# Local-attention layers: third group of the first FFN product moved to the output's PSUM banks, and a turned probability unit copied behind each maximum

## The chip, the cores and the metric

The kernel runs on one NeuronCore of a Trainium2 chip. The metric is the device time of one launch in microseconds (us). Before the change it is 3528.7 us, the median of 3 runs (3528.33 to 3528.79).

## What is computed

The reference is a chain of two blocks over 8 sequences of 512 rows with 256 features: a Mamba branch and an FP4-quantized FFN on a layer norm of the input, then block-sparse attention and two local-attention layers on a layer norm of the result. The change touches the local-attention layers alone. Cut to that part:

```python
def _layer(x, wqkv, qs, ksc, wo, lg, lb, w1, b1, w2, b2):      # called for l = 0, 1
    q, k, v = split(shift_token(x) @ wqkv)                     # 8 heads of 64
    q, k = rotary_xpos(l2norm(q) * qs, l2norm(k) * ksc)
    o = local_attention(q, k, v)       # windows of 128 rows; each sees itself and the one before
    x = x + o @ wo
    h = layer_norm(shift_token(x)) * lg + lb
    a, g = split(h @ w1 + b1)                                  # 682 columns each
    return x + (a * gelu(g)) @ w2 + b2
```

## The kernel before

`local_attention_layers` writes every engine's program by hand and orders them with semaphores; nothing is scheduled by a tool. It works on one batch (512 rows, four tiles of 128) at a time: 2 layers x 8 batches are 16 passes of `body`. In 15 of them (`more` is true) the body also prepares the next batch `n`, from its projection to its first scores, between the steps of its own batch `it`. The sixteenth has no next batch.

**PSUM.** All eight banks (128 x 512 fp32 each) are taken: `ps_s` has four, `ps_t` two, `ps_o` two. `ps_s` holds scores, raw q and k and the first FFN product; `ps_t` holds transposes and the product with `wo`; `ps_o` holds v, the attention output and, as `ps_y`, the second FFN product.

**Attention.** A unit is two heads of one window of 128 queries: 16 units u in 8 pairs s. For each pair TensorE writes scores into bank u % 4 (`score`, L2241 and L2249), VectorE takes the negated row maximum (`maxima`, L1989), ScalarE the exponential with its row sum (`exponents`, L2124), VectorE the reciprocals of a pair's sums (`inverses`, L2007), GpSimd scales (`scale_rows`, L1884), TensorE turns the scaled unit into bank u % 2 of `ps_t` (`turn_p`, L2261), VectorE copies it to SBUF (`take_p`, L2015), and TensorE weighs v with it (`weigh`, L2280). Units with window 0 see 128 columns a head (units 0, 1, 8, 9, "narrow"), the others 256. The stages are staggered: in step s TensorE does `score(s)`, `turn_p(s-2)`, `weigh(s-3)`, and VectorE does `inverses(s-1)`, `maxima(s)` for units 2s and 2s+1, `take_p(s-2)` for units 2s-4 and 2s-3. `turn_p` of unit u waits until unit u-2 has been copied, since both use the same bank of `ps_t`. The first two pairs of a batch are scored in the body of the batch before.

**First FFN product.** After the layer norm (`hn`, turned to `hT`) comes the loop over j = 0 to 5 at L2357 to L2369. Group j is the product for 128 columns of a (`a`=0) and 128 of g (`a`=1); j = 5 holds the 42 columns that are left of both in one bank. `pair(j)` gives banks 2 and 3 of `ps_s` to even j and banks 0 and 1 to odd j. ScalarE takes gelu of the g half (L2177, L2180), VectorE adds the bias to the a half and multiplies (`hid`, L2073). Group j may therefore start only when `hid` of group j-2 is done:

```python
                for j in range(JC):
                    if j >= 2:
                        pe.wait_ge(hid_ready.s, hid_ready.at(it, j - 1))
```

From j = 2 on, TensorE follows each group with the transposes of one tile of the next batch's q and k (`turn_qk`, L2230), which ScalarE and VectorE copy out (`take_q` L2130, `take_k` L1982). Then follow half of the second FFN product (`down_rows`, L2292), the next batch's first scores, and the other half.

**VectorE around it.** Ahead of its first `hid` VectorE has the next batch's `rotate(n, 2)`, `rotate(n, 3)`, `squares(n, 2)`, `squares(n, 3)`. `squares` (L1975, L1978) writes the sums of squares; it waits until GpSimd's `inverse_norms` (a power, L1867) of the tile before has read them. GpSimd runs `turn_heads` (L1861), `inverse_norms` (L1867) and `scale_heads` (L1874) tile by tile.

Of the kernel before, what the change touches and what calls it, by code (L numbers as in the profile page):

```python
# [7 lines left out]
ALU = mybir.AluOpType  # L8
# [1639 lines left out]
def local_attention_layers(nc, io, W, stream, base_dram, out, NB):  # L1648
# [15 lines left out]
    with ExitStack() as ctx:  # L1664
# [118 lines left out]
        def nk(u):  # L1783
            return 1 if UNIT[u][0] == 0 else 2
# [4 lines left out]
        def layers(eng, first, body):  # L1789

            first(0)
            for l in range(L):
# [5 lines left out]
                else:  # L1798
                    body(l, NB - 1, l * NB + NB - 1, None, None)

        def halves(ap):
            return ap.rearrange("p (h d) -> p h d", h=NH)

# [134 lines left out]
        def _(dve):  # L1938
# [43 lines left out]
                dve.tensor_copy(kT[:, :, t * P:(t + 1) * P], ps_t[:, 1, :].rearrange("p (c n) -> p c n", c=IC))\  # L1982
                    .then_inc(kT_ready.s, 1)

            def maxima(it, s):
                for u in (2 * s, 2 * s + 1):
                    w = 2 * P * nk(u)
                    dve.wait_ge(scores.s, scores.at(it, u + 1))
                    dve.tensor_reduce(negmax[:, u, :], ps_s[:, u % 4, 0:w].rearrange("p (h n) -> p h n", h=2),  # L1989
                                      AX.X, ALU.max, negate=True).then_inc(max_ready.s, 1)  # L1990

            def masked_maxima(it, s):

# [12 lines left out]
                dve.wait_ge(exp_ready.s, exp_ready.at(it, 2 * s + 2))  # L2006
                dve.reciprocal(inv[:, 2 * s:2 * s + 2, :], den[:, 2 * s:2 * s + 2, :]).then_inc(inv_ready.s, 1)  # L2007

            def take_p(it, s):
                for u in (2 * s, 2 * s + 1):  # L2010
                    w = 2 * P * nk(u)
                    dve.wait_ge(p_turned.s, p_turned.at(it, u + 1))
                    if u >= 8:
                        dve.wait_ge(pv_done.s, pv_done.at(it, u // 2 - 3))
                    dve.tensor_copy(pt[:, u % 8, 0:w], ps_t[:, u % 2, 0:w]).then_inc(pt_ready.s, 1)  # L2015

            def first(it):
                for t in range(TT):
# [9 lines left out]
            def body(l, b, it, nl, nb):  # L2028
                n, more = it + 1, nl is not None
                for s in range(AHEAD, PAIRS + TURN_LAG):  # L2030
                    if s <= PAIRS:
                        inverses(it, s - 1)
                    if s < PAIRS:
                        maxima(it, s)
                    take_p(it, s - TURN_LAG)
                if more:
                    for t in range(2):
                        rotate(nl, n, t)
                        squares(n, t)

                dve.wait_ge(wo_done.s, wo_done.at(it, 1))
                dve.wait_ge(xr_in.s, xr_in.at(it, 16))
                dve.wait_ge(xa2_ready.s, xa2_ready.at(it, 0))
                dve.wait_ge(hn_ready.s, hn_ready.at(it, 0))
                for half in (slice(P, D), slice(0, P)):
                    dve.tensor_tensor(xa[:, :, half], ps_x[:, :, half], xr[:, :, half], ALU.add).then_inc(xa_ready.s, 1)

                st.turn(it)
                dve.wait_ge(xa_ready.s, xa_ready.at(it, 2))
                for t in range(TT):  # L2050
                    st.done(dve.bn_stats(stats[:, t, 0:6], xa[:, t, 0:P]))
                dve.wait_ge(shifted.s, shifted.at(it, 1))
                for t in range(TT):
                    st.done(dve.bn_stats(stats[:, t, 6:12], xsh[:, t, :]))
                dve.wait_ge(st.s, st.at(2 * TT))
                st.done(dve.memset(tick[:, :], 0.0))
                for t in range(TT):
                    dve.bn_aggr(mv[:, t, :], stats[:, t, :]).then_inc(mv_ready.s, 1)
                dve.wait_ge(rstd_ready.s, rstd_ready.at(it, 1))
                for t in range(TT):  # L2060
                    for half, src in enumerate((xa[:, t, 0:P], xsh[:, t, :])):
                        dve.tensor_scalar(hn[:, t, half * P:(half + 1) * P], src, mv[:, t, 0:1], rstd[:, t:t + 1],
                                          ALU.subtract, ALU.mult).then_inc(hn_ready.s, 1)
                if more:
                    rotate(nl, n, 2)
                    rotate(nl, n, 3)
                    squares(n, 2)
                    squares(n, 3)

                for j in range(JC):  # L2070
                    m = jj(j)
                    dve.wait_ge(gl_ready.s, gl_ready.at(it, j + 1))
                    dve.scalar_tensor_tensor(hid[0:m, j, :], ps_s[0:m, pair(j), :], b1_cols[0:m, l, 0, j:j + 1],  # L2073
                                             gl[0:m, j % 2, :], ALU.add, ALU.mult).then_inc(hid_ready.s, 1)
                    if more and j >= JC - TT:
                        take_k(n, j - JC + TT)
                if more:
                    for s in range(AHEAD):
                        masked_maxima(n, s)
                    inverses(n, 0)  # L2080
                dve.wait_ge(y_done.s, y_done.at(it, 1))
                dve.wait_ge(xa2_ready.s, xa2_ready.at(it, 1))
                dve.wait_ge(stored.s, stored.at(it, 0))
                dve.tensor_tensor(xo[:, :, :], ps_y, xa2[:, :, :], ALU.add).then_inc(xo_ready.s, 1)
                st.end()
# [4 lines left out]
        def _(act):  # L2090
# [53 lines left out]
            def body(l, b, it, nl, nb):  # L2144
                n, more = it + 1, nl is not None
                for s in range(AHEAD, PAIRS):
                    exponents(it, s)
                    if s == HALF + PV_LAG - 1:
                        take_o(it, 0)
                if more:  # L2150
                    take_x(n)
                    square(n, 0)
                take_o(it, 1)
                if more:
                    square(n, 1)
                if l == L - 1:
                    act.wait_ge(stored.s, stored.at(it, 0))
                    act.dma_start(xo[:, :, :], base_dram[b].rearrange("(t p) d -> p t d", p=P)).then_inc(base_in.s, 16)
                if more:
                    take_v(n, 0)  # L2160
                    take_v(n, 1)
                    square(n, 2)
                    take_v(n, 2)
                    square(n, 3)
                for k in range(DC):
                    act.wait_ge(h_turned.s, h_turned.at(it, k + 1))
                    act.activation(hT[:, k, :], ps_t[:, k, :], ACT.Identity, bias=ln_cols[:, l, k, 1:2],
                                   scale=ln_cols[:, l, k, 0:1]).then_inc(hT_ready.s, 1)
                if more:
                    take_v(n, 3)  # L2170
                for j in range(JC):
                    m = jj(j)
                    act.wait_ge(ag_proj.s, ag_proj.at(it, j + 1))
                    if j >= 2:
                        act.wait_ge(hid_ready.s, hid_ready.at(it, j - 1))
                    if j < JC - 1:
                        act.activation(gl[:, j % 2, :], ps_s[:, pair(j) + 1, :], ACT.Gelu, bias=b1_cols[:, l, 1, j:j + 1])\  # L2177
                            .then_inc(gl_ready.s, 1)
                    else:
                        act.activation(gl[0:m, j % 2, :], ps_s[64:64 + m, pair(j), :], ACT.Gelu, bias=b1_tail[64:64 + m, l, 1, JC - 1:JC])\  # L2180
                            .then_inc(gl_ready.s, 1)
                    if more and j >= JC - TT:
                        take_q(n, j - JC + TT)
                if more:
                    for s in range(AHEAD):
                        exponents(n, s)
                if l == L - 1:
                    act.wait_ge(xo_ready.s, xo_ready.at(it, 1))
                    act.dma_start(out[b].rearrange("(t p) d -> p t d", p=P), xo[:, :, :]).then_inc(stored.s, 16)
# [4 lines left out]
        def _(pe):  # L2194
# [116 lines left out]
            def body(l, b, it, nl, nb):  # L2311
# [42 lines left out]
                    project_v(n, 3)  # L2354
                pe.wait_ge(hT_ready.s, hT_ready.at(it, DC))
                for j in range(JC):
                    if j >= 2:  # L2357
                        pe.wait_ge(hid_ready.s, hid_ready.at(it, j - 1))
                    elif more:
                        pe.wait_ge(raw_ready.s, raw_ready.at(n, TT - 1 + j))  # L2360

                    for a in range(2 if j < JC - 1 else 1):
                        at = a * FULL + j * P if j < JC - 1 else 2 * FULL
                        for k in range(DC):
                            last = pe.matmul(ps_s[:, pair(j) + a, :], w_1[:, k, at:at + P], hT[:, k, :],  # L2365
                                             start=(k == 0), stop=(k == DC - 1))
                    last.then_inc(ag_proj.s, 1)
                    if more and j >= JC - TT:
                        turn_qk(n, j - JC + TT)  # L2369
                if more:  # L2370
                    pe.wait_ge(v_ready.s, v_ready.at(n, TT))
                down_rows(it, (0, 2))
                if more:
                    pe.wait_ge(qT_ready.s, qT_ready.at(n, TT))
# [93 lines left out]
```

## Time and profile before

| | |
|---|---|
| median of 3 runs | 3528.7 us |
| the profiled execution | 3527.94 us |
| its span | 3526.2 us |
| TensorE matmuls busy | 3201.3 us (91%) |
| TensorE weight loads busy | 1865.3 us (53%) |
| VectorE busy | 2495.2 us (71%) |
| ScalarE busy | 1764.6 us (50%) |
| GpSimd busy | 1581.5 us (45%) |

The local layers fill the span from about 2016 us on. Columns of a timeline row: start in us, duration in us, engine, line, operation, output<-input, shapes, count; in brackets the idle time of the engine just before, and what ended it. PE is TensorE's matmuls, PEld its weight loads, DVE VectorE, ACT ScalarE, POOL GpSimd. Every fp32 matmul or transpose of the program stands as two records. The end of a matmul in the records is modelled, its start is recorded.

### The profile page before, as it was taken

The numbers are of one execution on the slowest core, as the hardware profiler recorded it, in microseconds if no ns is written. First come the engines' busy times: TensorE is split into PE (matmuls) and PEld (weight loads), VectorE is DVE, ScalarE is ACT, GpSimd is POOL, SyncE is SP. The second block draws the span as 40 slices with busy tenths as digits, with TensorE's granted clock in tenths as the row PEclk, the third lists the DMA queues.
The fourth block names the chain that finished last, engine by engine and source line by source line (L and its number), as shares of the span: only waits on it lengthen the run. The fifth ranks groups of instructions, "written<-read, shape, count | busy, mean of one in ns | idle before, by whom it ended". The sixth has DMA issues, their size and how long they took to land. (4 is left out here: it accounts for less than half of the span.)

```text
span 3526.2 us, 50669 instructions
## 1 busy us (share of the span) xinstructions
PE 3201.3 (91%) x16204; PEld 1865.3 (53%) x16204; DVE 2495.2 (71%) x3778; ACT 1764.6 (50%) x4156; POOL 1581.5 (45%) x974
## 2 busy tenths in 40 slices
PE   1799999989999876999999889999999999999997
PEld 1245454444544433666666546665666566666655
DVE  6499999999999995777777555555555555555553
ACT  1585767768576751556655433333333333333332
POOL 0456666666666662000000064444555555555552
PEclk9899999999999998999999889999999999999999
DMA  1466666757666672211000000000001100000000
GB/s 51 155 225 223 227 237 216 253 205 238 222 225 238 215 268 89 73 34 36 24 24 18 31 1 18 18 18 18 18 18 36 48 25 24 24 24 19 23 18 18
DMA packets 146655, 343.31 MB, mean 97 GB/s; under 512 B 14898, under 2 KB 78470, under 8 KB 146582
## 3 DMA queue, kind: packets, MB, share of 16 engines
q1 hardware_dynamic: 138134, 334.02, 27.9%
q10 hardware_dynamic: 8448, 8.39, 0.7%
q8 instruction: 37, 0.61, 0.1%
q14 instruction: 36, 0.29, 0.0%
HBM read 320.87 MB, written 21.50 MB: 97 GB/s over the span
## 5 line engine op out<-in xcount | busy, mean ns | idle before, releaser
L581 POOL TENSOR_TENSOR hb<-bcB,du 128x1024 f32<-128x1024 f32 x256 | 601.3, 2351 | 318.0 <-DVE hb L681 278.6
L670 DVE TENSOR_TENSOR_SCAN ps_dA<-ps_dA,hb 128x1024 f32<-128x1024 f32 x256 | 585.8, 2288 | 62.7 <-ACT ps_dA L831 62.4
L1053 PE MATMUL ps_y<-hb,ident 128*128 128x512 f32 x1024 | 496.4, 613 | 71.0 <-DVE hb L681 71.0
L1884 POOL TENSOR_TENSOR c_pr<-c_pr,c_inv 128x512 f32<-128x512 f32 (+1 forms) x256 | 233.4, 933 | 396.5 <-DVE c_inv L2007 394.6
L1053 PEld LDWEIGHTS ps_y<-hb,ident 128*128 128x128 f32 x1024 | 188.2, 193 | 310.4 <-issue 183.7
L1418 ACT ACTIVATE b_pr<-b_ps_s,b_negmax 128x256 f32<-128x256 f32 (+1 forms) x512 | 263.8, 527 | 163.2 <-DVE b_negmax L1332 160.9
L2124 ACT ACTIVATE c_pr<-c_ps_s,c_negmax 128x256 f32<-128x256 f32 (+1 forms) x512 | 222.0, 449 | 228.1 <-DVE c_negmax L1989 153.1
L2365 PE MATMUL c_ps_s<-c_hT,c_w 128*128 128x512 f32 x704 | 319.3, 599 | 17.4 <-DVE c_hid L2073 16.6
L831 ACT ACTIVATE ps_dA<-delta,a_neg 128x511 f32<-128x511 f32 x512 | 330.1, 676 | 1.1
L681 DVE TENSOR_TENSOR hb<-ps_dA,bcC 128x1024 f32<-128x1024 f32 x256 | 312.1, 1219 | 6.1 <-issue 0.3
L1861 POOL TENSOR_TENSOR c_q_cos<-c_q_cos,c_q_sin 128x1024 f32<-128x1024 f32 x64 | 150.7, 2355 | 236.5 <-DVE c_q_sin L1968 236.5
L1332 DVE TENSOR_REDUCE b_negmax<-b_ps_s 128x2 f32<-128x512 f32 (+1 forms) x320 | 204.2, 681 | 70.6 <-PE b_ps_s L1489 69.6
L1276 POOL TENSOR_TENSOR b_xb<-b_xb,b_o_bias 128x1024 f32<-128x1024 f32 x8 | 18.8, 2346 | 495.8 <-DMA b_xb<-x_scratch 495.8
L2211 PE MATMUL c_ps_s<-c_w_qkv,c_xT 128*128 128x512 f32 x512 | 237.9, 608 | 0.7 <-ACT c_xT L2097 0.7
L2365 PEld LDWEIGHTS c_ps_s<-c_hT,c_w 128*128 128x128 f32 x704 | 128.3, 191 | 175.4 <-issue 144.4
L1503 PE MATMUL b_ps_t<-ident,b_pr 128*128 128x128 f32 x1280 | 189.2, 285 | 24.7 <-DVE b_pt L1354 12.7
L2073 DVE SCALAR_TENSOR_TENSOR c_hid<-c_ps_s,c_b_cols,c_gl 128x512 f32<-128x512 f32 x96 | 70.3, 745 | 185.9 <-ACT c_gl L2177 166.3
L1867 POOL TENSOR_TENSOR c_rn<-c_ssc,c_mhalf 128x16 f32<-128x16 f32 x64 | 186.2, 2910 | 33.8 <-DVE c_ssc L1978 33.4
L2103 ACT ACTIVATE c_sq<-c_ps_s 128x512 f32<-128x512 f32 x128 | 69.5, 595 | 255.2 <-PE c_ps_s L2211 255.2
L1503 PEld LDWEIGHTS b_ps_t<-ident,b_pr 128*128 128x128 f32 x1280 | 136.6, 141 | 113.7 <-DVE b_pt L1354 55.6
L1489 PE MATMUL b_ps_s<-b_kf,b_qm 32*128 32x256 f32 (+1 forms) x1024 | 177.0, 459 | 0.9 <-ACT b_kf L1391 0.9
L2177 ACT ACTIVATE c_gl<-c_ps_s,c_b_cols 128x512 f32<-128x512 f32 x80 | 55.1, 689 | 238.8 <-PE c_ps_s L2365 238.8
(241 smaller groups left out, 6320.7 us busy)
## 6 DMA issues: line engine op xcount, KB each, us to landing
bcB<-bc_scratch SPq DMA_DIRECT2D x256, 512.0 KB, 4.4
bcC<-bc_scratch SPq DMA_DIRECT2D x256, 512.0 KB, 4.6
c_x<-stream_scratch SPq DMA_DIRECT2D x16, 512.0 KB, 5.3
c_xr<-stream_scratch SPq DMA_DIRECT2D x16, 512.0 KB, 4.2
xn<-in_x_dram SPq DMA_DIRECT2D x8, 512.0 KB, 5.1
xr<-in_x_dram SPq DMA_DIRECT2D x8, 512.0 KB, 5.1
x_scratch<-xr SPq DMA_DIRECT2D x8, 512.0 KB, 7.0
b_x<-x_scratch SPq DMA_DIRECT2D x8, 512.0 KB, 4.3
```

The source lines that it names most:

```text
L581: pool.tensor_tensor(hb[:, s % RING, :, :], bcB[:, s % ROWS, :, :], bc(du[:, c % 2, :].unsqueeze(1), [P, NG, T]), ALU.mult)\
L670: dve.tensor_tensor_scan(flat(h_all), flat(h_all), flat(tile), 0.0, ALU.mult, ALU.add)\
L681: dve.tensor_tensor(tile, h_all, bcC[:, s % ROWS, :, :], ALU.mult).then_inc(weighed.s, 1)
L831: last = act.activation(dA[:, s % 2, n, 1:], delta[:, c, 1:], ACT.Exp, scale=a_neg[:, c, g * NG + n:g * NG + n + 1])
L1053: last = pe.matmul(ps_y[:, :], W["ident"][:, :], hb[:, r % RING, i, :], start=False, stop=(g == GROUPS - 1 and i == terms - 1))
L1332: dve.tensor_reduce(negmax[:, u, 0:heads], ps_s[:, u % 4, :].rearrange("p (h n) -> p h n", h=heads), AX.X, ALU.max, negate=True).then_inc( ...
L1418: last = act.activation(pr[:, u % 8, cols], ps_s[:, u % 4, cols], ACT.Exp, bias=negmax[:, u, i:i + 1], accum_out=den[:, qt, h:h + 1])
L1503: last = pe.transpose(ps_t[:, u % 2, k * P:(k + 1) * P], pr[:, u % 8, k * P:(k + 1) * P], W["ident"][:, :])
L1884: pool.tensor_tensor(rows, rows, bc(inv[:, u, :].unsqueeze(2), [P, 2, w]), ALU.mult)\
L2124: last = act.activation(pr[:, u % 6, i * w:(i + 1) * w], ps_s[:, u % 4, i * w:(i + 1) * w], ACT.Exp, scale=-1.0 if s < AHEAD else 1.0, bia ...
L2211: last = pe.matmul(ps_s[:, pair(t) + a, :], xT[:, k, t * P:(t + 1) * P], w_qkv[:, k, a * INNER:(a + 1) * INNER], start=(k == 0), stop=(k = ...
L2365: last = pe.matmul(ps_s[:, pair(j) + a, :], w_1[:, k, at:at + P], hT[:, k, :], start=(k == 0), stop=(k == DC - 1))
```

## The change

Two edits, both in the local layers.

1. A helper `ag(j, a)` names the bank of each group. j = 2 goes to the two banks of `ps_o`; the later groups move up by one in the alternation over `ps_s`. With it go the waits: j = 2 waits for the next batch's v to be out of `ps_o` (`v_ready`, a wait that stood ahead of the second product) and for no `hid`; j = 3, 4, 5 wait for `hid` of groups 0, 1, 3; the second product waits for `hid` of group 2.
2. VectorE's two maxima and two copies of a step are interleaved: maximum 2s, copy 2s-4, maximum 2s+1, copy 2s-3.

```diff
+        def ag(j, a):
+
+            return ps_o[:, a, :] if j == 2 else ps_s[:, pair(j + (j > 2)) + a, :]
+
...
                 for s in range(AHEAD, PAIRS + TURN_LAG):
                     if s <= PAIRS:
                         inverses(it, s - 1)
-                    if s < PAIRS:
-                        maxima(it, s)
-                    take_p(it, s - TURN_LAG)
+                    for i in range(2):
+                        if s < PAIRS:
+                            maximum(it, 2 * s + i)
+                        take_p(it, 2 * (s - TURN_LAG) + i)
...
-                    dve.scalar_tensor_tensor(hid[0:m, j, :], ps_s[0:m, pair(j), :], b1_cols[0:m, l, 0, j:j + 1],
+                    dve.scalar_tensor_tensor(hid[0:m, j, :], ag(j, 0)[0:m, :], b1_cols[0:m, l, 0, j:j + 1],
...
-                        act.activation(gl[:, j % 2, :], ps_s[:, pair(j) + 1, :], ACT.Gelu, bias=b1_cols[:, l, 1, j:j + 1])\
+                        act.activation(gl[:, j % 2, :], ag(j, 1), ACT.Gelu, bias=b1_cols[:, l, 1, j:j + 1])\
...
                 for j in range(JC):
-                    if j >= 2:
-                        pe.wait_ge(hid_ready.s, hid_ready.at(it, j - 1))
+
+                    if j >= 3:
+                        pe.wait_ge(hid_ready.s, hid_ready.at(it, (1, 2, 4)[j - 3]))
+                    elif more and j == 2:
+                        pe.wait_ge(v_ready.s, v_ready.at(n, TT))
                     elif more:
                         pe.wait_ge(raw_ready.s, raw_ready.at(n, TT - 1 + j))
...
-                            last = pe.matmul(ps_s[:, pair(j) + a, :], w_1[:, k, at:at + P], hT[:, k, :],
+                            last = pe.matmul(ag(j, a), w_1[:, k, at:at + P], hT[:, k, :],
...
-                if more:
-                    pe.wait_ge(v_ready.s, v_ready.at(n, TT))
+                pe.wait_ge(hid_ready.s, hid_ready.at(it, 3))
                 down_rows(it, (0, 2))
```

TensorE, first FFN product in the body's loop, groups j = 1 to 3 before (`c_hT` is the normed input turned, `c_w` the weights, `c_raw` the semaphore of `rotate`):

```order
L2365 MATMUL c_ps_s<-c_hT,c_w 128x512 [waits c_raw]
L2365 MATMUL c_ps_s<-c_hT,c_w 128x512 x3
L2358 ISA
L2365 MATMUL c_ps_s<-c_hT,c_w 128x512 [waits c_hid]
L2365 MATMUL c_ps_s<-c_hT,c_w 128x512 x3
L2230 MATMUL c_ps_t<-ident,c_qr 128x128 [waits c_qr_ready]
L2230 MATMUL c_ps_t<-ident,c_qr 128x128 x7
L2358 REGISTER_ALU
L2365 MATMUL c_ps_s<-c_hT,c_w 128x512 [waits c_hid]
```

and in the changed kernel:

```order
L2371 MATMUL c_ps_s<-c_hT,c_w 128x512 [waits c_raw]
L2371 MATMUL c_ps_s<-c_hT,c_w 128x512 x3
L2371 MATMUL c_ps_o<-c_hT,c_w 128x512 [waits c_v_ready]
L2371 MATMUL c_ps_o<-c_hT,c_w 128x512 x3
L2233 MATMUL c_ps_t<-ident,c_qr 128x128 [waits c_qr_ready]
L2233 MATMUL c_ps_t<-ident,c_qr 128x128 x7
L2362 ISA
L2371 MATMUL c_ps_s<-c_hT,c_w 128x512 [waits c_hid]
```

The wait for `hid` has moved from group 2 to group 3; the number of matmuls and their order are the same.

VectorE, attention, step s = 7 of the body's loop before (units 14 and 15 get their maximum, units 10 and 11 are copied):

```order
L2007 RECIPROCAL c_inv<-c_den 128x4 [waits c_exp]
L1988 REGISTER_ALU
L1989 TENSOR_REDUCE c_negmax<-c_ps_s 128x2 [waits c_scores]
L1988 REGISTER_ALU
L1989 TENSOR_REDUCE c_negmax<-c_ps_s 128x2 [waits c_scores]
L2014 REGISTER_ALU [waits c_p_turned]
L2015 COPY c_pt<-c_ps_t 128x512 [waits c_pv]
L2015 COPY c_pt<-c_ps_t 128x512 [waits c_pv,c_p_turned]
```

and in the changed kernel:

```order
L2010 RECIPROCAL c_inv<-c_den 128x4 [waits c_exp]
L1991 REGISTER_ALU
L1992 TENSOR_REDUCE c_negmax<-c_ps_s 128x2 [waits c_scores]
L2016 REGISTER_ALU [waits c_p_turned]
L2017 COPY c_pt<-c_ps_t 128x512 [waits c_pv]
L1991 REGISTER_ALU
L1992 TENSOR_REDUCE c_negmax<-c_ps_s 128x2 [waits c_scores]
L2017 COPY c_pt<-c_ps_t 128x512 [waits c_pv,c_p_turned]
```

The first copy and its wait for the turned unit now stand ahead of the second maximum; the second copy is still last.

## Rows read from the trace of the kernel before

**Rows 1.** Busy time by stretch: us, PE, PEld, DVE, ACT, POOL busy (count), PEclk, DMA, GB/s

```profile
2246.40:2338.10 91.70, 89.96 (x470) 55.86 (x469) 52.56 (x121) 34.38 (x99) 46.58 (x31) 1.00 0.06 17
```

**Rows 2.** Waits of PE from 2000 us on: us in total, times, longest us

```profile
PE c_ps_s L2365 <- DVE c_hid L2073: 16.6, 15, 1.2
...
PE c_ps_t L2261 <- DVE c_pt L2015: 10.3, 32, 0.5
```

**Rows 3.** Timeline of PE, first FFN product of one batch

```profile
2306.15 7.13 PE L2365 MATMUL c_ps_s<-c_hT,c_w 128*128 128x512 f32 x16
2314.38 3.70 PE L2365 MATMUL c_ps_s<-c_hT,c_w 128*128 128x512 f32 x8 [1.10 <-DVE c_hid L2073]
2317.91 1.04 PE L2230 MATMUL c_ps_t<-ident,c_qr 128*128 128x128 f32 x8
...
2329.12 1.04 PE L2230 MATMUL c_ps_t<-ident,c_qr 128*128 128x128 f32 x8
```

**Rows 4.** Timeline of PEld, the same place

```profile
2311.83 0.19 PEld L2365 LDWEIGHTS c_ps_s<-c_hT,c_w 128*128 128x128 f32 x1 [0.24 <-issue]
2312.26 0.19 PEld L2365 LDWEIGHTS c_ps_s<-c_hT,c_w 128*128 128x128 f32 x1 [0.24 <-issue]
2314.37 0.30 PEld L2365 LDWEIGHTS c_ps_s<-c_hT,c_w 128*128 128x128 f32 x2 [1.93 <-DVE c_hid L2073]
2314.91 0.19 PEld L2365 LDWEIGHTS c_ps_s<-c_hT,c_w 128*128 128x128 f32 x1 [0.24 <-issue]
```

**Rows 5.** Timeline of DVE, the same place

```profile
2311.75 1.22 DVE L1975 TENSOR_REDUCE c_ss<-c_sq 128x16 f32<-128x1024 f32 x1 [3.09 <-POOL c_rn L1867]
...
2313.58 1.40 DVE L2073 SCALAR_TENSOR_TENSOR c_hid<-c_ps_s,c_b_cols,c_gl 128x512 f32<-128x512 f32 x2
```

**Rows 6.** Timelines of ACT and POOL, the same place

```profile
2306.19 0.60 ACT L2108 ACTIVATE c_v<-c_ps_o 128x512 f32<-128x512 f32 x1 [0.17 <-PE c_ps_o L2219]
...
2309.88 0.69 ACT L2177 ACTIVATE c_gl<-c_ps_s,c_b_cols 128x512 f32<-128x512 f32 x1 [1.79 <-PE c_ps_s L2365]
...
2321.19 1.90 POOL L1874 TENSOR_TENSOR c_qr<-c_q_cos,c_rn 128x1024 f32<-128x1024 f32 x1
```

**Rows 7.** Timeline of PE, attention of the same batch

```profile
2256.90 1.22 PE L2261 MATMUL c_ps_t<-ident,c_pr 128*128 128x128 f32 x8 [0.19 <-DVE c_pt L2015]
...
2267.54 1.09 PE L2261 MATMUL c_ps_t<-ident,c_pr 128*128 128x128 f32 x8
...
2269.67 1.23 PE L2261 MATMUL c_ps_t<-ident,c_pr 128*128 128x128 f32 x8 [0.45 <-DVE c_pt L2015]
```

**Rows 8.** Timeline of PEld, the same two places

```profile
2257.46 0.42 PEld L2261 LDWEIGHTS c_ps_t<-ident,c_pr 128*128 128x128 f32 x4 [0.18 <-issue]
...
2270.24 0.42 PEld L2261 LDWEIGHTS c_ps_t<-ident,c_pr 128*128 128x128 f32 x4 [0.18 <-issue]
```

**Rows 9.** Timeline of DVE, steps s = 3 and s = 5 to 9 of the same batch

```profile
2256.07 1.28 DVE L2015 COPY c_pt<-c_ps_t 128x512 f32<-128x512 f32 x2
...
2260.78 1.29 DVE L1989 TENSOR_REDUCE c_negmax<-c_ps_s 128x2 f32<-128x512 f32 x2 [0.79 <-PE c_ps_s L2249]
...
2267.64 1.29 DVE L1989 TENSOR_REDUCE c_negmax<-c_ps_s 128x2 f32<-128x512 f32 x2 [0.34 <-PE c_ps_s L2249]
2268.85 1.28 DVE L2015 COPY c_pt<-c_ps_t 128x512 f32<-128x512 f32 x2
...
2273.51 1.29 DVE L2015 COPY c_pt<-c_ps_t 128x512 f32<-128x512 f32 x2 [1.79 <-PE c_ps_t L2261]
```

**Rows 10.** Timelines of ACT and POOL, exponentials and scaling of the last pair

```profile
2269.28 0.47 ACT L2124 ACTIVATE c_pr<-c_ps_s,c_negmax 128x256 f32<-128x256 f32 x1
...
2270.59 2.04 POOL L1884 TENSOR_TENSOR c_pr<-c_pr,c_inv 128x512 f32<-128x512 f32 x2 [1.18 <-DVE c_inv L2007]
```

**Rows 11.** Timeline of PE, turns of pair 7: batch of rows 3, then the last batch

```profile
2272.73 1.09 PE L2261 MATMUL c_ps_t<-ident,c_pr 128*128 128x128 f32 x8
...
3464.48 0.65 PE L2261 MATMUL c_ps_t<-ident,c_pr 128*128 128x128 f32 x4 [0.17 <-POOL c_pr L1884]
```

More of the change, by code:

```diff
@@ L1983, in take_k, with maximum @@
                     .then_inc(kT_ready.s, 1)
[L1985 to L1990, printed above, removed]
+            def maximum(it, u):
+                w = 2 * P * nk(u)
+                dve.wait_ge(scores.s, scores.at(it, u + 1))
+                dve.tensor_reduce(negmax[:, u, :], ps_s[:, u % 4, 0:w].rearrange("p (h n) -> p h n", h=2),
+                                  AX.X, ALU.max, negate=True).then_inc(max_ready.s, 1)
             def masked_maxima(it, s):
@@ L2007, in inverses, with take_p @@
                 dve.reciprocal(inv[:, 2 * s:2 * s + 2, :], den[:, 2 * s:2 * s + 2, :]).then_inc(inv_ready.s, 1)
[L2009 to L2015, printed above, removed]
+            def take_p(it, u):
+                w = 2 * P * nk(u)
+                dve.wait_ge(p_turned.s, p_turned.at(it, u + 1))
+                if u >= 8:
+                    dve.wait_ge(pv_done.s, pv_done.at(it, u // 2 - 3))
+                dve.tensor_copy(pt[:, u % 8, 0:w], ps_t[:, u % 2, 0:w]).then_inc(pt_ready.s, 1)
             def first(it):
@@ L2176, in body @@
                     if j < JC - 1:
-                        act.activation(gl[:, j % 2, :], ps_s[:, pair(j) + 1, :], ACT.Gelu, bias=b1_cols[:, l, 1, j:j + 1])\
+                        act.activation(gl[:, j % 2, :], ag(j, 1), ACT.Gelu, bias=b1_cols[:, l, 1, j:j + 1])\
                             .then_inc(gl_ready.s, 1)
                     else:
-                        act.activation(gl[0:m, j % 2, :], ps_s[64:64 + m, pair(j), :], ACT.Gelu, bias=b1_tail[64:64 + m, l, 1, JC - 1:JC])\
+                        act.activation(gl[0:m, j % 2, :], ag(j, 0)[64:64 + m, :], ACT.Gelu, bias=b1_tail[64:64 + m, l, 1, JC - 1:JC])\
                             .then_inc(gl_ready.s, 1)
```

## The prediction

> **What bounds the kernel now.** First the busy time by stretch, cut at the period of the local layers. The timeline repeats every 91.68 us (the stalled matmul group starts at 2131.01, 2222.69, 2314.38). In one period TensorE is busy 89.96 of 91.70 us, VectorE 52.56, GpSimd 46.57, ScalarE 34.40, and the granted clock is 1.00 [rows 1]. So TensorE sets the period, and there are 1.74 us of it to win by the matmul rows. Next the list of TensorE's waits, which names them: 16.6 us in 15 waits for `hid` in the first FFN product, 10.3 us in 32 waits for a copied unit in attention [rows 2]. 15 passes have a next batch, and 32 is twice for each of 16 passes. The two edits aim at these two lines.
>
> Then the timelines, to see which event each wait really ends on. TensorE runs groups 0 and 1 from 2306.15, then stands 1.10 us and starts group 2 at 2314.38 [rows 3]. VectorE's two `hid` start at 2313.58, directly behind `squares` of the last tile, which itself started at 2311.75 after 3.09 us of waiting for GpSimd's power [rows 5]. The gelu that the first `hid` needs ran at 2309.88 [rows 6]; what is late is VectorE, whose queue holds `squares` ahead of `hid`. The bank rule (group 2 reuses group 0's banks) hands that lateness to TensorE.
>
> **Edit 1, group 2 in the output's banks.** Removed: the wait of group 2 for `hid` 0. Added: a wait for the next batch's last v. ScalarE copies it from 2306.19 on for 0.60 us, done at 2306.79 [rows 6], over 6 us ahead of group 2: free. 
> How much is the stall? The matmul row says 1.10 us. The weight loads give the starts instead: they come every 0.43 us (2311.83, 2312.26), and the load in front of group 2 is 2312.26. Unhindered, the first of group 2 would be at 2312.69 and the third at 2313.55; it is at 2314.91 [rows 4]. The difference, 1.36 us, is what TensorE falls behind. Check: from the first matmul of group 0 to the first transpose behind group 2 it takes 2317.91 - 2306.15 = 11.76 us [rows 3], and 24 matmuls at 0.43 are 10.3 us plus 0.1 for the first pair of loads. I take 1.36 us. The trace supports this reading by itself; the Trainium skill (Perfetto Trace Analysis, Tensor Engine Instruction) says why the two differ: a matmul's reported end is estimated from its size, not observed. Going by reported idle the term would be 15 x 1.10 = 16.5 us; by the starts it is 15 x 1.36 = **20.4 us**.
>
> Is another wait late next? Group 3 now needs `hid` 0. It starts about 3.44 us (eight matmuls) plus 0.88 us (eight transposes) after group 2, at 2313.1 + 4.3 = 2317.4; `hid` 0 ends by 2314.3 [rows 5], 3 us earlier. Groups 4 and 5 need `hid` 1 and `hid` 3, one group more of distance than before or the same. The last transposes of q and k, which move from 2329.12 [rows 3] to 2327.8, need GpSimd's scaled tile, done at 2321.19 + 1.90 = 2323.09 [rows 6]: 4.7 us of slack. The second product waits for `hid` 2, several us old. The first scores of the next batch and all that follows hang on TensorE's own progress and move with it. In the last pass VectorE has no `squares` to do and TensorE shows no wait there: no gain. So the 1.36 us stays won in 15 passes.
>
> **Edit 2, a copy behind each maximum.** The two waits are at step s = 4 (turning units 4 and 5) and s = 8 (units 12 and 13) [rows 7]. Take s = 8. Unit 12 waits for the copy of unit 10, unit 13 for that of unit 11. VectorE's maxima begin at 2267.64, the copies at 2268.85, one slot being about 0.605 us, so the copies end at 2269.53 and 2270.13 [rows 9]. Unit 12 starts at 2269.67, 0.14 us after its copy [rows 7], and the loads of unit 13 at 2270.24, 0.11 us after its own [rows 8]. Now interleave. The copy of unit 10 moves up by 0.6 us and unit 12 needs not wait. But the copy of unit 11 stays fourth of four and ends at the same 2270.13: unit 13 starts at 2270.24 as before, and TensorE waits there instead. The same at s = 4: the copies end by 2256.07 + 1.28 = 2257.35 [rows 9] and unit 5 starts at 2257.46 [rows 8]. The wait changes its name and keeps its length: **0 gain**.
>
> It has small costs. (a) At s = 7 the first copy now needs unit 10 turned just after its turn began at 2267.54 [rows 7]. A turn is seen by VectorE 0.78 us after its start (2272.73 [rows 11] to 2273.51 [rows 9]), so at 2268.32, while the slot opens at 2268.25: 0.08 us later, handed on to unit 13. (b) The second maximum comes 0.6 us later, so the second exponential starts up to 0.4 us later: ScalarE needs about 0.9 us for a unit, and it started unit 15 at 2269.28 right behind unit 14 [rows 10]. Now the first copy starts at 2268.33, the second maximum at 2268.93, and with 0.68 us of duration it ends at 2269.6: 0.35 us later for the exponential. GpSimd's scaling of the pair (2270.59 to 2272.63 [rows 10]) comes 0.35 to 0.4 us later with it, and unit 15, turned half a microsecond after 2272.73 [rows 11], has them just in time (2273.0 against 2273.2). In steps 5 to 7 VectorE idled 0.79 to 0.34 us for TensorE in front of its maxima [rows 9], which takes up such a delay. At s = 3 I find 0.04 us that reach unit 5. (c) A copy followed directly by a maximum occurs nowhere in the trace. Between full overlap as in the rows (slots of 0.605 against 0.68 us of duration [rows 9]) and none, it costs 0 to 0.08 us, once in each of the two chains; I take 0, since maximum to copy and copy to copy both show the overlap. Together 0.12 us x 16 = **+1.9 us**, bounds 0 and 16 x 0.3 = 4.8. As a gain the bound is the whole line of rows 2, 10.3 us. In the last pass nothing covers the late pair: unit 15 waits for GpSimd there [rows 11], so its delay goes to the end once, **+0.4 us**.
>
> **Sum.** -20.4 + 1.9 + 0.4 = -18.1 us. The profiled execution, 3527.9 us (span 3526.2 and 1.7 around it), becomes 3509.8. It lay 0.8 us under the median, so against the median the forecast is 3528.7 - 18.1 = **3510.6 us**, 0.5% faster. About 0.2% (7 us) is what a measurement of this kernel can tell from no change.
>
> **Rivals.**
> 1. *The copies do release TensorE.* For: the wait line of rows 2 names the copies, and the first of each pair moves up 0.6 us. Against: the second unit starts 0.11 us after the last copy in both places [rows 8]. Instead of +1.9 us it would give -10.3: 3528.7 - 20.4 - 10.3 + 0.4 = 3498. Chance 7%.
> 2. *Part of edit 1's gain is handed to a later wait*, say half of it, at group 3 or in the next batch's attention, where exponential, reciprocal and scaling must follow the scores. Then 3528.7 - 10.2 + 2.3 = 3521. Against: slacks of 3 and 4.7 us, and attention hangs on its own scores. Chance 9%.
> 3. *The later exponentials become the bound* (the other side). Place: steps 2 to 7 of attention, where `inverses` stands in front of the next maximum on VectorE and waits for the exponential of the second unit, now 0.4 us later. If each of six steps loses 0.4 us and TensorE's scores follow, 16 x 6 x 0.4 = 38 us come on top: 3528.7 - 20.4 + 38 = 3547. It decides once the delay exceeds VectorE's idle before its maxima; more than 1.3 us a batch must get through to be slower at all. Against: idles of 0.79 and 0.34 us [rows 9]. Chance 3%.
> 4. *The change does not do what it says*: group 2 finds another wait as late (its weights and `hT` are there, v is out) and only the interleaving's 2.3 us are left, 3531. Chance 3%.
>
> **How the numbers follow.** The forecast has 78%. Its own range goes from reported idle alone with the worst interleaving (-16.5 + 4.8 + 0.4: 3517.4) to the full 1.36 us and free interleaving (-20.4 + 0.4: 3508.7). To keep 8 in 10 I reach a little toward rivals 1 and 2: 3504 to 3517.5. Faster by over 0.2% (under 3521.6): forecast, rival 1 and most of rival 2, 0.92. Within 0.2%: rest of 2 and 4, 0.05. Slower: 0.03.
>
> **What the profile after would show.** No wait for `hid` in the list of TensorE's waits; groups 0 to 2 in one row of 24 matmuls lasting some 10.6 us; a period of 90.3 to 90.5 us with granted clock 1.00. VectorE's idle before `squares` still about 3.1 us. In attention the waits for copies stay near 10 to 13 us in total but stand in front of units 5 and 13, and unit 15 does not wait. Wrong would be: a period under 90.0 us (rival 1), or a new wait of over 0.5 us on TensorE between group 3 and the next first scores (rival 2).

## The result and the profile after

The changed kernel takes 3513.48 us (median of 6 runs, 3511.22 to 3515.98); over its six runs the kernel before takes 3528.74 us (3524.65 to 3536.03). The ratio is 0.9955, with a 95% interval of 0.9944 to 0.9966: 16 us or 0.45% faster, between 12 and 20 us (the two medians lie 15.3 us apart). The forecast was 3510.6 us within 3504.0 to 3517.5, and a ratio of 0.9949. Two executions among the experiments below, one of e5 with 5651.7 us and one of e8 with 6788.1 us, were slow ones and stand in no median.

The profiled execution took 3512.49 us with a span of 3510.6 us. The list of TensorE's waits after the change, from 2000 us on (us in total, times, longest us), against [rows 2]:

```profile
PE c_ps_t L2233 <- POOL c_qr L1878: 13.4, 3, 5.5
PE c_ps_t L2264 <- DVE c_pt L2017: 12.3, 32, 0.6
```

The line for `hid`, 16.6 us before, is gone. The waits of transposes for GpSimd's scaled q and k, now first, lie in the first batch's preparation. The line for the copied units is still there, 32 times, and has grown from 10.3 to 12.3 us.

The first FFN product on PE, against [rows 3]:

```profile
2305.67 7.13 PE L2371 MATMUL c_ps_s<-c_hT,c_w 128*128 128x512 f32 x16
2312.64 3.60 PE L2371 MATMUL c_ps_o<-c_hT,c_w 128*128 128x512 f32 x8
2316.07 1.04 PE L2233 MATMUL c_ps_t<-ident,c_qr 128*128 128x128 f32 x8
...
2327.28 1.04 PE L2233 MATMUL c_ps_t<-ident,c_qr 128*128 128x128 f32 x8
```

and its weight loads, against [rows 4]:

```profile
2311.78 0.19 PEld L2371 LDWEIGHTS c_ps_s<-c_hT,c_w 128*128 128x128 f32 x1 [0.24 <-issue]
2312.21 0.19 PEld L2371 LDWEIGHTS c_ps_o<-c_hT,c_w 128*128 128x128 f32 x1 [0.24 <-issue]
2312.64 0.19 PEld L2371 LDWEIGHTS c_ps_o<-c_hT,c_w 128*128 128x128 f32 x1 [0.24 <-issue]
```

The loads run through from bank to bank at 0.43 us. From the first matmul of group 0 to the first transpose it takes 10.40 us instead of 11.76: 1.36 us less. VectorE's `hid` is as late as ever, and nobody waits for it:

```profile
2311.28 1.22 DVE L1979 TENSOR_REDUCE c_ss<-c_sq 128x16 f32<-128x1024 f32 x1 [3.09 <-POOL c_rn L1871]
...
2313.11 1.40 DVE L2076 SCALAR_TENSOR_TENSOR c_hid<-c_ps_s,c_b_cols,c_gl 128x512 f32<-128x512 f32 x2
```

Attention of the same batch on PE, against [rows 7]:

```profile
2256.06 0.66 PE L2264 MATMUL c_ps_t<-ident,c_pr 128*128 128x128 f32 x4
2256.94 0.63 PE L2264 MATMUL c_ps_t<-ident,c_pr 128*128 128x128 f32 x4 [0.22 <-DVE c_pt L2017]
...
2268.60 0.65 PE L2264 MATMUL c_ps_t<-ident,c_pr 128*128 128x128 f32 x4
2269.80 0.63 PE L2264 MATMUL c_ps_t<-ident,c_pr 128*128 128x128 f32 x4 [0.55 <-DVE c_pt L2017]
```

Units 4 and 12 start without a wait now; units 5 and 13 wait instead.

The product with `wo` marks the period. Its starts on PE, two in layer 0 and two in layer 1:

```profile
2282.50 7.07 PE L2338 MATMUL c_ps_t<-c_w_o,c_oT 128*128 128x256 f32 x32
...
2372.91 7.07 PE L2338 MATMUL c_ps_t<-c_w_o,c_oT 128*128 128x256 f32 x32
...
2915.70 7.07 PE L2338 MATMUL c_ps_t<-c_w_o,c_oT 128*128 128x256 f32 x32
...
3006.21 7.07 PE L2338 MATMUL c_ps_t<-c_w_o,c_oT 128*128 128x256 f32 x32
```

The period is 90.41 us in layer 0 and 90.51 in layer 1; before it was 91.68 in both. That is one reading the forecast didn't have: layer 1 gains 0.1 us less.

Two measures are useful from here on. The period of the local layers repeats to 0.01 or 0.02 us within a layer of each kernel, away from the change of layer. "The local stretch" is the span less the start of the first scores: 3526.2 - 2062.76 = 1463.4 us before, 3510.6 - 2064.72 = 1445.9 us after, 17.5 us less. The stages ahead of it run identical code in all kernels of this study, yet their end lay between 2059.4 and 2065.6 us in the profiled executions. In this pair it was 2.0 us later in the changed kernel, which is why the spans differ by 15.6 us only. The stretch has one uncertainty that the period lacks. In the last batch TensorE stands idle before the first FFN product (9.1 us and, after eight transposes, 0.9 us) and starts it at the lower of its two granted clocks (0.50 in the rows, 1.2 GHz). The row of groups 0 and 1 lasts 8.70 us in e1, 9.02 in the changed kernel and 10.13 in e8, with a mean granted clock of 0.82, 0.79 and 0.66 over its first 9 us.

### The profile page after: what moved, and what is told of

The parts are those of the page before. It is cut to its first block and busy times, and to the rows that moved or that the text cites. A ratio compares the mean times of both kernels' runs of the same rounds, so it can differ in the third digit from the quotient of the medians.

```text
span 3510.6 us, 50669 instructions
## 1 busy us (share of the span) xinstructions
PE 3200.0 (91%) x16204; PEld 1867.5 (53%) x16204; DVE 2497.7 (71%) x3778; ACT 1771.1 (50%) x4156; POOL 1581.7 (45%) x974
## 5 line engine op out<-in xcount | busy, mean ns | idle before, releaser
L2371 PE MATMUL c_ps_s<-c_hT,c_w 128*128 128x512 f32 x576 | 260.9, 599 | 0.9 <-ACT c_hT L2170 0.9
L2017 DVE COPY c_pt<-c_ps_t 128x512 f32<-128x512 f32 (+1 forms) x256 | 155.2, 616 | 24.5 <-PE c_ps_t L2264 23.9
L2295 PE MATMUL c_ps_o<-c_w,c_hid 128*128 128x256 f32 x768 | 172.4, 381 | 0.0
L2371 PEld LDWEIGHTS c_ps_s<-c_hT,c_w 128*128 128x128 f32 x576 | 105.4, 191 | 123.1 <-issue 121.1
```

The costliest lines, as they stand in the source:

```text
L2295: last = pe.matmul(ps_y[:, t, :], hid[:, j, t * P:(t + 1) * P], w_2[:, j, :], start=(j == 0), stop=(j == JC - 1))
L2371: last = pe.matmul(ag(j, a), w_1[:, k, at:at + P], hT[:, k, :], start=(k == 0), stop=(k == DC - 1))
```

## The experiments

All experiments are held against the kernel before. Periods and stretches are from each one's profiled execution:

| kernel | median us | ratio, 95% interval | period, layer 0 / 1 | local stretch |
|---|---|---|---|---|
| before | 3528.7 | | 91.68 / 91.68 | 1463.4 |
| changed | 3513.5 | 0.9955 [0.9944, 0.9966] | 90.42 / 90.52 | 1445.9 |
| e1 edit 1 alone | 3508.0 | 0.9946 [0.9933, 0.9960] | 90.31 / 90.32 | 1442.8 |
| e2 edit 2 alone | 3531.0 | 1.0006 [0.9997, 1.0015] | 91.78 / 91.89 | 1466.4 |
| e3 banks, old wait kept | 3529.6 | 1.0001 [0.9992, 1.0010] | 91.68 / 91.68 | 1463.4 |
| e4 squares behind hid 0 | 3506.9 | 0.9937 [0.9921, 0.9952] | 90.31 / 90.31 | 1442.7 |
| e5 edit 1, x turned first | 3501.7 | 0.9932 [0.9907, 0.9957] | 89.83 / 89.83 | 1435.8 |
| e6 edit 1, copies in step 3 | 3507.9 | 0.9946 [0.9926, 0.9967] | 90.06 / 90.06 | 1439.0 |
| e7 edit 1, copies in step 7 | 3518.4 | 0.9973 [0.9963, 0.9984] | 90.79 / 90.90 | 1452.4 |
| e8 both edits, one wait a copy | 3510.5 | 0.9960 [0.9942, 0.9977] | 90.33 / 90.33 | 1444.8 |
| e9 e5 and e6 together | 3499.8 | 0.9918 [0.9904, 0.9931] | 89.57 / 89.57 | 1431.9 |

Medians of 3 to 11 runs can't tell neighbours in this list apart (e1, e4, e5 and e6 overlap, and so do e8 and the changed kernel); the periods do. A ratio has its own runs of the kernel before beside it and is not the quotient of two medians of this table; the two differ by up to 0.1%.

**e1, edit 1 alone.** The changed kernel with VectorE's loop over s, and the two helpers that it calls, as before. Against the changed kernel:

```diff
-                    for i in range(2):
-                        if s < PAIRS:
-                            maximum(it, 2 * s + i)
-                        take_p(it, 2 * (s - TURN_LAG) + i)
+                    if s < PAIRS:
+                        maxima(it, s)
+                    take_p(it, s - TURN_LAG)
```

> Edit 1 alone: group 2 in the output's banks, maxima and copies in the old order. My theory: all of the gain is edit 1's, 1.36 us in each of 15 batches, and edit 2 costs about 0.11 us a batch. The period of the local layers (91.68 us before, 90.42 with both edits) becomes 90.32 us, and the time is 20 us under before, about 2 us under the changed kernel. Waits for copies are again in front of units 4 and 12, 0.19 and 0.45 us. Rival (the copies released TensorE and carry part of the gain): the period stays above 90.5 us and the gain is under 16 us.

Measured: period 90.31 to 90.32 us, local stretch 20.6 us shorter than before and 3.1 us shorter than in the changed kernel. In its timeline unit 12 waits 0.45 us for a copy again, and the waits for copies add up to 10.3 us, as before. All of the gain is edit 1's.

**e2, edit 2 alone.** The changed kernel with the first FFN product as before.

> Edit 2 alone: the interleaved maxima and copies, the first FFN product as before. My theory: the wait only moves from units 4 and 12 to units 5 and 13, and 0.11 us a batch are lost: period 91.79 us, time 1 to 3 us over before. The group-2 stall stays at 1.10 us of idle. Rival (the copies release TensorE): period 91.0 us, time 8 to 10 us under before.

Measured: period 91.78 us in layer 0 and 91.89 in layer 1, local stretch 3.0 us longer. The runs' times show no difference that can be told from none (1.0006, 0.9997 to 1.0015), the periods show the loss. The two stalls of each batch on PE stand at units 5 and 13:

```profile
2254.38 0.63 PE L2260 MATMUL c_ps_t<-ident,c_pr 128*128 128x128 f32 x4 [0.22 <-DVE c_pt L2013]
...
2267.24 0.63 PE L2260 MATMUL c_ps_t<-ident,c_pr 128*128 128x128 f32 x4 [0.55 <-DVE c_pt L2013]
```

The effects add: -1.36 and +0.10 us of period in layer 0 make the changed kernel's -1.26.

**e3, the banks without the wait's removal.** e1 plus

```diff
+                    if j == 2:
+                        pe.wait_ge(hid_ready.s, hid_ready.at(it, 1))
```

> Edit 1 with the old wait kept: group 2 goes to the output's banks but still waits for hid of group 0. My theory: it is the wait alone, not the banks as such: period 91.68 us and the 1.10 us of idle in front of group 2 as before, time as before within 1 us. Rival (matmuls, gelu or hid run better when they lie in other banks): the period falls below 91.5 us with the wait still there.

Measured: period 91.68 us, and the old idle with the new bank in the row on PE:

```profile
2306.67 7.13 PE L2374 MATMUL c_ps_s<-c_hT,c_w 128*128 128x512 f32 x16
2314.90 3.70 PE L2374 MATMUL c_ps_o<-c_hT,c_w 128*128 128x512 f32 x8 [1.10 <-DVE c_hid L2077]
```

The banks as such are worth nothing. They only allow the wait to be left out.

**e4, the other end of the same wait.** The kernel before, with one call moved on VectorE:

```diff
                     squares(n, 2)
-                    squares(n, 3)
...
                     dve.scalar_tensor_tensor(hid[0:m, j, :], ps_s[0:m, pair(j), :], b1_cols[0:m, l, 0, j:j + 1],
                                              gl[0:m, j % 2, :], ALU.add, ALU.mult).then_inc(hid_ready.s, 1)
+                    if more and j == 0:
+                        squares(n, 3)
```

> No bank is changed; VectorE does the last tile's squares behind the first hid instead of ahead of it. My theory: group 2 was late because hid 0 stood behind squares on VectorE, so this cures it as well: hid 0 starts about 2.8 us earlier, no idle in front of group 2, period 90.32 us, 20 us under before, as edit 1 alone. The scaled tile comes at the same time, since squares waits for GpSimd anyhow. Rival (the reuse of two banks is itself too tight, hid 0 would come too late behind its gelu): idle of 0.3 us or more stays in front of group 2 or moves to group 3.

Measured: period 90.31 us, local stretch 20.7 us shorter. On VectorE `hid` 0 and `squares` have changed places, and both follow what they need at once:

```profile
2307.76 0.75 DVE L2072 SCALAR_TENSOR_TENSOR c_hid<-c_ps_s,c_b_cols,c_gl 128x512 f32<-128x512 f32 x1 [1.94 <-ACT c_gl L2178]
2308.91 1.22 DVE L1975 TENSOR_REDUCE c_ss<-c_sq 128x16 f32<-128x1024 f32 x1 [0.40 <-POOL c_rn L1867]
```

and TensorE runs its three groups in one row:

```profile
2303.31 10.56 PE L2366 MATMUL c_ps_s<-c_hT,c_w 128*128 128x512 f32 x24
```

The two pairs of banks were never too few. An instruction that waits 3.09 us for GpSimd stood in the same queue ahead of one that was ready first: before the change the gelu for `hid` 0 was done at 2309.88 + 0.69 = 2310.57 [rows 6], 1.18 us before `squares` started.

**e5, other work in front of the wait.** e1 plus, on TensorE:

```diff
+                    if s == PAIRS and more:
+                        pe.wait_ge(exp_ready.s, exp_ready.at(it, UNITS - 2))
+                        pe.wait_ge(x_in.s, x_in.at(it, 16))
+                        turn_x(n)
                     if s < PAIRS + TURN_LAG:
                         turn_p(it, s - TURN_LAG)
-                    if s == PAIRS and more:
-                        pe.wait_ge(exp_ready.s, exp_ready.at(it, UNITS - 2))
-                        pe.wait_ge(x_in.s, x_in.at(it, 16))
-                        turn_x(n)
```

> Edit 1 alone, and in step 8 TensorE turns the next batch's x ahead of units 12 and 13 instead of behind them. My theory: the wait at step 8 is for the fourth slot on VectorE (the copy of unit 11), so other work of TensorE's (0.87 us) in front of it hides it. Turning takes place with both copies done; about 0.66 us are free, some 0.15 us come back as a wait of unit 15 for GpSimd: period 89.8 us against 90.32 with edit 1 alone, time 7 to 8 us under it. Rival (TensorE's wait there belongs to the chain through exponential and scaling, which moves along): unit 12 or 15 waits as long, period stays at 90.2 us or above.

Measured: period 89.83 us, 0.48 less than e1, and local stretch 7.0 us shorter. TensorE turns x from 2266.80 on and then units 12 and 13 in one row without a wait:

```profile
2266.80 1.09 PE L2203 MATMUL c_ps_s<-ident,c_x 128*128 128x128 f32 x8
2267.72 1.04 PE L2265 MATMUL c_ps_t<-ident,c_pr 128*128 128x128 f32 x8
2268.69 1.09 PE L2284 MATMUL c_ps_o<-c_pt,c_v 128*64 128x128 f32 x16
2269.72 1.26 PE L2265 MATMUL c_ps_t<-ident,c_pr 128*128 128x128 f32 x8
```

The last row, the pair of units 14 and 15, takes 0.17 us longer than the 1.09 us of [rows 11]: what comes back, as expected.

**e6, both copies of step 3 one slot earlier.** e1 plus

```diff
+                    if s in (3,):
+                        maxima(it, s, (0,))
+                        take_p(it, s - TURN_LAG)
+                        maxima(it, s, (1,))
+                        continue
```

> Edit 1 alone, and in step 3 VectorE does maximum 6, copy 2, copy 3, maximum 7. My theory: what the interleaving left in place is the last copy's fourth slot; one slot earlier (0.6 us) it is out of the way, and step 5's idle (0.79 us) takes the later exponential. No wait at unit 4 or 5, 0.3 to 0.4 us a batch: period 89.9 to 90.0 us. Rival (the delayed exponential, 0.8 us later, becomes the bound): a wait for GpSimd or for scores appears in steps 4 to 6 and the period is 90.3 us or more.

Measured: period 90.06 us, 0.26 less than e1, a little short of 0.3 to 0.4. The wait at units 4 and 5 is gone (16 waits for copies are left, all at step 8). The later exponential isn't quite free: the pair of units 6 and 7 takes 1.19 us instead of 1.09 on PE.

**e7, the same in step 7.** As e6 with `(7,)` for `(3,)`.

> Edit 1 alone, and in step 7 VectorE does maximum 14, copy 10, copy 11, maximum 15. My theory: unit 13 starts 0.5 us earlier, but the exponential of unit 15 starts about 1 us later, its scaling ends at about the place where TensorE would be 1 us earlier, so unit 15 waits about 1 us: a net loss, period 90.7 to 90.9 us. This is where the slack ends that hid the later exponentials. Rival (the exponential's lateness is hidden here as well): period 89.8 us.

Measured: period 90.79 us in layer 0, 0.48 more than e1, and 90.90 in layer 1. That is the loss expected, though it comes as two waits of about 0.35 us and not as one of 1 us. The waits for copies fall to 3.0 us in total, and a new line stands above them in the list of PE's waits:

```profile
PE c_ps_t L2270 <- POOL c_pr L1888: 12.5, 33, 1.2
...
PE c_ps_t L2270 <- DVE c_pt L2019: 3.0, 16, 0.3
```

Its places in one batch are units 14 and 15, which now stand behind GpSimd's scaling:

```profile
2270.25 0.66 PE L2270 MATMUL c_ps_t<-ident,c_pr 128*128 128x128 f32 x4 [0.36 <-POOL c_pr L1888]
2271.25 0.66 PE L2270 MATMUL c_ps_t<-ident,c_pr 128*128 128x128 f32 x4 [0.34 <-POOL c_pr L1888]
```

So the mechanism of rival 3, a later exponential that becomes the bound, exists at the last pair. It needs one slot of 0.6 us more of delay than edit 2 gives.

**e8, the copies' second wait left out.** The changed kernel without

```diff
-                if u >= 8:
-                    dve.wait_ge(pv_done.s, pv_done.at(it, u // 2 - 3))
```

> Both edits, and VectorE's copies wait only for the turned unit, not also for the weighing that freed their slot in pt (TensorE does that weighing earlier in its own order, so the turned unit implies it). Theory B (the turned unit itself comes too late for the moved copy): the period stays 90.42 in layer 0, and the copy of unit 10 still starts over 0.65 us behind the maximum of unit 14.

Measured: 90.33 us in both layers, 0.09 and 0.19 us less than the changed kernel. Step 7 on VectorE, first in layer 0 of the changed kernel, where the first copy starts 0.68 us behind its maximum:

```profile
2267.09 0.69 DVE L1992 TENSOR_REDUCE c_negmax<-c_ps_s 128x2 f32<-128x512 f32 x1 [0.33 <-PE c_ps_s L2252]
2267.77 0.69 DVE L2017 COPY c_pt<-c_ps_t 128x512 f32<-128x512 f32 x1
```

then in layer 1, 0.80 us behind it:

```profile
2900.17 0.69 DVE L1992 TENSOR_REDUCE c_negmax<-c_ps_s 128x2 f32<-128x512 f32 x1 [0.33 <-PE c_ps_s L2252]
2900.97 0.69 DVE L2017 COPY c_pt<-c_ps_t 128x512 f32<-128x512 f32 x1
```

and in layer 0 of e8, 0.61 us behind it:

```profile
2264.00 0.69 DVE L1992 TENSOR_REDUCE c_negmax<-c_ps_s 128x2 f32<-128x512 f32 x1 [0.33 <-PE c_ps_s L2250]
2264.61 0.68 DVE L2015 COPY c_pt<-c_ps_t 128x512 f32<-128x512 f32 x1
```

Theory A holds: the turned unit was there in time, and without the second wait the copy starts in its slot. But it was there only just in time, and that is half of the cause. In e8 a copy that has nothing but the turned unit to wait for (unit 14, behind 1.46 us of idle time) starts 0.69 us after its turn, and the slot of unit 10 opens 0.71 us after its own (2263.90 to 2264.61).

```profile
2263.90 1.09 PE L2262 MATMUL c_ps_t<-ident,c_pr 128*128 128x128 f32 x8
...
2269.09 1.09 PE L2262 MATMUL c_ps_t<-ident,c_pr 128*128 128x128 f32 x8
...
2269.78 1.29 DVE L2015 COPY c_pt<-c_ps_t 128x512 f32<-128x512 f32 x2 [1.46 <-PE c_ps_t L2262]
```

The register instruction that carries the wait for the turned unit has no slack to hide in. Two places in the changed kernel show it. In step 6 unit 8 has the same two waits, but it is narrow and turned sooner, and its copy starts 0.61 us behind its maximum in every batch:

```profile
2263.77 0.66 PE L2264 MATMUL c_ps_t<-ident,c_pr 128*128 128x128 f32 x4
2263.87 0.69 DVE L1992 TENSOR_REDUCE c_negmax<-c_ps_s 128x2 f32<-128x512 f32 x1 [0.49 <-PE c_ps_s L2252]
2264.48 0.41 DVE L2017 COPY c_pt<-c_ps_t 128x256 f32<-128x256 f32 x1
```

The first seven batches of a layer run in a loop of the program, the eighth is written out behind it. In the eighth of layer 0 unit 10, as wide and as late as ever and with both waits, starts 0.61 us behind its maximum too:

```profile
2719.03 1.09 PE L2264 MATMUL c_ps_t<-ident,c_pr 128*128 128x128 f32 x8
2719.13 0.69 DVE L1992 TENSOR_REDUCE c_negmax<-c_ps_s 128x2 f32<-128x512 f32 x1 [0.33 <-PE c_ps_s L2252]
2719.74 0.68 DVE L2017 COPY c_pt<-c_ps_t 128x512 f32<-128x512 f32 x1
```

What is missing there is the register instruction. The copies' line has four of them in a batch of the loop (the first two rows, window 2620:2640) and none in the eighth batch (the third, window 2710:2730):

```profile
L2016 DVEq ALU_OP  x3: 40/40/40, 2629.3 to 2634.6; - x3
L2016 DVEq FUSED_REGOPS  x1: 46/46/46, 2625.9 to 2625.9; - x1
L2016 DVEq EVENT_SEMAPHORE  x8: 21/21/21, 2715.9 to 2724.9; - x8
```

The delay of unit 10 is 0.07 us in the seven batches of layer 0's loop, 0.43 in the first of layer 1's and 0.18 to 0.19 in the next six. The local stretch is only 1.1 us shorter than the changed kernel's, since the row of groups 0 and 1 in the last batch, at the lower clock for longer, takes 1.1 us more.

**e9, both cures.** e5 and e6 together, without edit 2.

> Edit 1 with both cures that helped alone: TensorE turns the next batch's x ahead of units 12 and 13, and VectorE does both copies of step 3 behind one maximum. Edit 2 is left out. If the two waits are independent, as my theory has it, the savings add: period 90.32 - 0.49 - 0.26 = 89.57 us, about 11 us under edit 1 alone and 13 us under the changed kernel. If the 0.15 us that step 3's order leaves at unit 7, or unit 15's wait for GpSimd, grow when TensorE is ahead, the period is 89.7 us or more.

Measured: 3499.79 us, ratio 0.9918 (0.9904 to 0.9931), 29 us under before and 14 under the changed kernel. The period is 89.57 us, as the sum says. The stretch of one period, with the columns of [rows 1]:

```profile
2154.70:2244.27 89.57, 89.57 (x470) 55.90 (x469) 52.53 (x121) 34.34 (x98) 46.60 (x31) 1.00 0.05 18
```

TensorE's records leave no idle time in it, at a granted clock of 1.00. That is not quite the floor: the turns of units 6 and 7 still last 1.19 us and those of units 14 and 15 1.26, against 1.09 without a delay, as in e6 and e5.

## Why the prediction was right, and where not

- **TensorE sets the period.** Right. In every kernel the period moved by what TensorE's stall moved, and at last fell to its busy time (e9). ScalarE's 34.40 and GpSimd's 46.57 us a period are 34.38 and 46.58 in [rows 1]; nothing hangs on them.
- **Edit 1, 1.36 us in each of 15 batches.** Right in size and cause: e1 gives 91.68 - 90.32 = 1.36 us and 20.6 us over the local stretch, against a term of 20.4. The reading by starts was the right one; the matmul rows' idle time (1.10 us) would have made it 16.5. So the Trainium skill's remark (Perfetto Trace Analysis, Tensor Engine Instruction) that a matmul's end is estimated mattered here by 0.26 us a stall. That the wait and not the bank is what counts is shown by e3, and that VectorE's queue order was the cause by e4.
- **No later wait takes its place.** Right: no wait for `hid` or for the scaled q and k appears behind group 2, and from the first matmul of group 0 to the last transposes it takes 21.61 us (2305.67 to 2327.28) instead of 22.97, the same 1.36 us less.
- **Edit 2 gains nothing, the wait changes units.** Right, by the timeline and by e2. The whole list line stayed, though the profile named the copies as its releaser and the first of each pair was moved up by 0.6 us.
- **Edit 2's cost, 1.9 us, and 0.4 in the last pass.** Right in size and place, with half of the cause missing.

  Up to the last product with `wo` the changed kernel loses 2.7 us against e1: 2.4 in the batches before and 0.3 in the last pass. The 0.3 us that its local stretch is longer on top of that are the row of groups 0 and 1 in the last batch (9.02 against 8.70 us); e2 against before shows the same (12.40 against 12.11 us with group 2 in the row).

  Step (a) said that the copy of unit 10 starts 0.08 us late, since a turn is seen 0.78 us after its start. It does start 0.07 us late in layer 0. But the 0.78 us came from a row that has the register instruction in it: a copy with one wait sees the turn after 0.69 us (e8), before its slot opens. So what step (a) put down to the turn is the register instruction behind it, and that this costs 0.19 us or more in layer 1 and nothing in the last batch of either layer is not in the forecast. Without that instruction edit 2 costs 0.02 us a batch (e8's period over e1's), where the forecast had 0.04 for unit 5. Before the change two maxima stood in front of the copy, and the instruction cost nothing: the first copy started 1.21 us after the first maximum, in its slot. Interleaving put the copy directly behind the first maximum.
- **Later exponentials are absorbed.** Right for edit 2: unit 15 was in time in the loop, and in the last pass it waited, as forecast (0.17 us of idle [rows 11] became 0.34). e7 shows how near the edge was.
- **The sum.** -18.1 us forecast, -17.5 in the local stretch, -16 by the ratio of the runs with 12 to 20 as the interval. Edit 1 gave 0.2 us more over the stretch than forecast and edit 2 cost 0.4 to 0.7 us more, so the sum owes little to luck.

Open: why the same instructions cost 0.12 us more in layer 1 than in layer 0, and 0.36 us more in its first batch. e8 shows that it goes away with the second wait, not what makes it differ. e4 and e5 were not run together, so whether edit 1's banks are needed at all in the fastest version wasn't tried.

## What to carry to other kernels

When a buffer's consumer is late, look at what stands ahead of it in its own queue. Moving the instruction that is ready first ahead of one that waits for a third engine (e4) gave as much as a new place for the buffer (edit 1) and needs no other bank. When work is interleaved to free a waiting engine, ask which of the results the waiter needs last: unless that one moves up, the wait only changes its name, and other work placed in front of it (e5) is the better cure. Price a stall on TensorE by the starts of its weight loads, not by the idle time of its matmul rows.

## What the runs showed of the hardware that was not expected

- In a loop, a VectorE copy with two semaphores to wait for has a register instruction in front of it that carries the first wait. Where this condition is met just as the slot opens, the copy starts 0.07 us (layer 0) or 0.19 us (layer 1; 0.43 in its first batch) later behind the instruction ahead of it than in e8, where it has one wait and no such instruction. It costs nothing where the condition is met sooner (unit 8: 0.61 us behind its maximum), where another 0.6 us instruction lies between, as before the change, or in the batch outside the loop, which has no register instruction there (0.61 us).
- Copy followed by maximum overlaps as the other pairs of instructions do: the starts of four in a row in e8 lie 0.61, 0.60 and 0.59 us apart with durations of 0.68 or 0.69 us. The forecast had left 0 to 0.08 us open for it.
- With identical code ahead of them, the first scores came between 2059.4 and 2065.6 us of the span. A difference of 2 or 3 us between two single profiles of this kernel says nothing; the period of a loop does.
